# Softmax attention on TensorE: value products in groups of four slots instead of ones and twos

## The reference, cut to what matters

```python
q = (x @ Wq.T).reshape(B, S, H, hd).transpose(0, 2, 1, 3)     # k, v alike
att_rel_pos = jnp.einsum('bhsd,pd->bhsp', q, pos_emb_k)
att_idxs = jnp.clip(ar[None, :] - ar[:, None], -r, r - 1) % P  # r = 128, P = 256
att_pos = att_rel_pos[:, :, ar[:, None], att_idxs]
attn_val = jnp.einsum('bhqd,bhkd->bhqk', q, k)
att = jax.nn.softmax((attn_val + att_pos) * attn_scale, axis=-1)
y = jnp.einsum('bhqk,bhkd->bhqd', att, v)
```

## Time and profile before

| | us |
|---|---|
| median of three runs | 1145.63 |
| lowest and highest | 1142.08, 1151.29 |
| the profiled execution, its own time | 1143.02 |
| its span in the trace | 1141.1 |
| L1002, first to last start in the span | 439.5 to 898.0 |

### The profile page before, as it was taken

The page is one execution under the profiler, slowest core; times in us unless marked ns, Lnnn a source line. Parts: engine busy times, 40 slices in busy tenths (PEclk is TensorE's granted clock), DMA queues, the critical chain, the costliest instruction groups (busy, mean ns, idle before and its releaser), DMA issues. The chain is left out here.

```text
span 1141.1 us, 22305 instructions
## 1 busy us (share of the span) xinstructions
PE 1032.1 (90%) x7828; PEld 643.7 (56%) x7828; DVE 756.0 (66%) x1707; ACT 728.8 (64%) x1087; POOL 541.1 (47%) x707
## 2 busy tenths in 40 slices
PE   3699999999998758999999999999999889999997
PEld 2444444677785434555555555554444466878785
DVE  7135342478865566787788888877786257676766
ACT  1479988556555326777777777777775655545453
POOL 1257776575543231333355544444222277555564
PEclk9979999999999857999999999999999999999999
DMA  4621141544664497888888888887672576433333
GB/s 160 225 79 51 57 128 32 151 124 141 164 192 154 157 264 228 241 244 241 242 254 261 250 248 238 242 240 243 217 225 62 146 195 131 120 117 122 116 123 91
DMA packets 146430, 197.41 MB, mean 173 GB/s; under 512 B 33292, under 2 KB 113149, under 8 KB 146285
## 3 DMA queue, kind: packets, MB, share of 16 engines
q1 hardware_dynamic: 126254, 184.32, 52.7%
q0 software_dynamic: 20064, 11.66, 5.8%
HBM read 123.00 MB, written 72.74 MB: 172 GB/s over the span
## 5 line engine op out<-in xcount | busy, mean ns | idle before, releaser
L1089 DVE TENSOR_REDUCE a_part<-a_duo 128x2 f32<-128x1024 f32 (+3 forms) x256 | 215.3, 855 | 13.5 <-PE a_duo L962 11.9
L755 POOL DMA_DIRECT2D scr_y1c<-ys x240 | 118.9, 504 | 207.7 <-DVE ys L1070 204.8
L1082 DVE CUSTOM_DVE_ANT_0 a_band_sum<-a_duo,a_rel_raw 128x256 f32<-128x256 f32 (+2 forms) x320 | 131.4, 448 | 79.6 <-PE a_duo L962 59.2
L1526 POOL TENSOR_TENSOR f_hid_lo<-f_hid,att 128x512 fp32r<-128x512 f32 (+1 forms) x100 | 129.7, 1298 | 104.7 <-ACT att L1495 104.7
L706 ACT ACTIVATE a_probs<-a_duo 128x1024 f32<-128x1024 f32 x192 | 140.2, 828 | 25.5 <-PE a_duo L655 24.3
L975 PE MATMUL a_duo<-att 32*128 32x512 f32 (+3 forms) x672 | 138.1, 408 | 17.0 <-DVE a_part L1089 12.8
L962 PE MATMUL a_duo<-att 31*128 31x512 f32 (+3 forms) x672 | 144.8, 427 | 9.4 <-PEq L1131 4.3
L1042 ACT ACTIVATE a_rel<-a_rel_ps 128x384 f32<-128x384 f32 x240 | 117.5, 490 | 47.5 <-PE a_rel_ps L949 45.3
L1658 DVE TENSOR_TENSOR f_hid<-f_u,w_share 128x512 f32<-128x512 f32 (+1 forms) x168 | 116.3, 692 | 32.0 <-DMA w_share<-scr_cw 9.4
L644 POOL TENSOR_TENSOR a_probs<-a_probs,const 128x256 f32<-128x256 f32 x128 | 101.7, 811 | 60.9 <-ACT a_probs L706 60.8
L1526 POOL TENSOR_TENSOR f_hid_lo<-f_hid,f_hid_hi 128x512 fp32r<-128x512 f32 x68 | 87.9, 1292 | 79.7 <-ACT f_hid_hi L1495 79.6
(11 more groups left out here) (268 smaller groups left out, 2049.3 us busy)
## 6 DMA issues: line engine op xcount, KB each, us to landing
a_rel_raw<-scr_rel SPq DMA_DIRECT2D x128, 384.0 KB, 4.4
scr_rel<-a_rel SPq DMA_DIRECT2D x120, 384.0 KB, 3.6
w_share<-scr_cw SPq DMA_DIRECT2D x144, 128.0 KB, 3.1
w_share<-scr_cw SPq DMA_DIRECT2D x44, 256.0 KB, 3.2
scr_y1c<-ys POOLq DMA_DIRECT2D x240, 8.0 KB, 3.7
w_share<-scr_cw SPq DMA_DIRECT2D x20, 192.0 KB, 2.9
w_share<-scr_cw SPq DMA_DIRECT2D x16, 224.0 KB, 3.0
att<-scr_q SPq DMA_DIRECT2D x36, 96.0 KB
```

The costliest lines, as they stand in the source:

```text
L755: eng.dma_start(scr["y1c"][w, b, head, :, at:at + T // 4], sb["ys"][32 * (2 * hd + c) + HD * w:32 * (2 * hd + c) + HD * (w + 1), h % 2, :] ...
L1082: ins = dve.tensor_tensor_reduce(band_sum[:, m % 2, hd, 0:wide], both[:, hd, (a - 4 * x) * P:(b - 4 * x) * P], rel_raw[:, e % RING, hd, (a ...
L1089: ins = dve.tensor_reduce(part[:, h % 2, x, :, j % 4], both[:, :, lo * P:hi * P], AX.X, ALU.max, negate=True)
L1526: pool.tensor_tensor(hid_lo[0:m, n % 4, :], hid[0:m, n % 2, :], f32(hid_hi[0:m, n % 4, :]), ALU.subtract).then_inc(lo_ready, 1)
```

## The change

Values move between slots; no instruction is added or removed. Before, ten of the sixteen slots of a pair run one or two values, 2 in slots 0, 3, 5, 9, 12 and 14, and 1 in slots 1, 7, 8 and 10. Now four values run together at the end of each of the slots 2, 6, 10 and 14 (in slot 6 the values 0 to 3 of the pair, in slot 2 the last four of the pair before). VectorE's copy L1070 stands one slot later (slots 3 and 11 instead of 2 and 10).

```diff
-    VALUES = (2, 1, 0, 2, 0, 2, 0, 1, 1, 2, 1, 0, 2, 0, 2, 0)
+    VALUES = (0, 0, 4, 0) * 4
...
-                    while valued < min(n - 1 if n >= SLOTS else n // 16 * 16 + sum(VALUES[:n % 16 + 1]) - 3, SLOTS):
+                    while valued < min(n - 1 if n >= SLOTS else n // 16 * 16 + sum(VALUES[:n % 16 + 1]) - 4, SLOTS):
                         values(valued)
                         valued += 1
...
-                if (n - 3) % 8 == 7 and 0 <= n - 3 < SLOTS:
-                    h = (n - 3) // 8
+                if (n - 4) % 8 == 7 and 0 <= n - 4 < SLOTS:
+                    h = (n - 4) // 8
                     dve.wait_ge(pv_done, 8 * h + 8)
                     wait(dve, y_stored[h % 2], 128 * (h // 2))
                     dve.tensor_copy(ys[:, h % 2, :], acc[:, 0:QUARTER]).then_inc(y_saved, 1)
```

## The result

The changed kernel takes 1315.99 us (median of 4) against 1146.58 before: a ratio of 1.149, 95% interval 1.142 to 1.157. The direction was forecast, the size was not: +40 us forecast, +170 measured (1313.79 against 1143.02 in the profiled executions).

What follows compares the result with a forecast made beforehand. PE, DVE and ACT were taken as near each other, slots held by whoever is late. DVE, starved behind groups, adds 2.66 us a pair: 15.1 pairs give 40.2; 1143.0 + 40.2 - 0.5 = 1183 us, range 1160 to 1206.

Steps and rivals of the forecast that it cites:

- DVE is left without scores behind each group: Slots 2, 6, 10, 14: DVE idles a slot's length less 1.39 us; 5.45 us a pair after hiding two copies.
- The sum of a pair, 31.8 us: Stage, one pair: 22.99 DVE work + 5.45 + 1.96 + 1.4 = 31.8 us, against 29.14 before.
- The chain over L1107: Slots 3 and 11: next L949 waits for DVE's copy, DVE then for scores; 1.96 us a pair, stays.
- other idle time: DVE's remaining idle time in a pair: between 0 and about 3.2 us, taken as 1.4.
- The group cost of 0.13 us: PE's array-use change per value group; six fewer groups save 0.8 us a pair; rival that this decides: 1130.5 us, 5%.
- ACT's hold (the third rival): L1046 in slots 2, 6, 10 waits for a value's buffer; 0.5 us each, 23 more, 1206 us; 12%.
- so no clock is to be won: Stage: PE's granted clock is already 1.00, its upper level, so the change cannot raise it.
- L975's waits for L1089: Sign of being right: PE's L975 waits for DVE's maxima L1089 in most slots without values.
- The forecast of PE's busy time: Sign of being right: PE's busy time in a pair falls below 27 of 31.8 us.

## Why the prediction was right and where it failed

- **DVE is left without scores behind each group: right.** Its idle time there at full clock was 6.00 us a pair against 5.45.
- **The sum of a pair, 31.8 us: right for full clock.** 32.49 was measured, in a pair with 24.48 us of DVE work where the sum took 22.99 from a pair with less of the router's. The chain over L1107 left 0.82 and 0.60, 1.42 in all, of DVE idle time instead of 1.96; other idle time was 0.59 (32.49 - 24.48 - 6.00 - 1.42) instead of 1.4. That the total came so near is in part luck: two terms were 2.0 us too small together, two 1.4 too large. So 15.1 x (32.5 - 29.1) = 51 us are structure, where the forecast had 40. From copy to copy most pairs before take 29.3, by which it is 48. The run with 37 extra matmuls agrees: take off what its pairs are longer than 32.49, 0.86 x 15.1 = 13 us, and 1191 is left, against 1143 + 51 = 1194.
- **The group cost of 0.13 us: not decisive, as said.** By it groups of two would be 8 us slower than fours (four groups more a pair, 0.13 each, 16 pairs); they are 144 faster, and at full clock too a pair of theirs is shorter, 31.42 against 32.49.
- **ACT's hold (the third rival): refuted** by the two runs with seven buffers, above all the one at full clock. The prediction had the hold in three slots; by the code and the trace it is in four, slot 14 too. Hidden, it cost nothing.
- **The step that failed: "so no clock is to be won".** It asked only whether the clock could rise, and the sum then kept the prices of the earlier trace rows, all taken at 1.00, for a kernel that waits more. The clock fell to 0.73. Its own list had what was missing: L975's waits for L1089 in most slots without values. The other 170 - 51 = 119 us are this, some 8 us a pair: 41.1 against 32.5. The clock can account for it: at 0.73 it is at the lower level for 54% of the 540 us, 292 us, and half the clock can lose half of that at most, 146. The forecast of PE's busy time (below 27 us a pair) was the one that its profile refuted first: 36.02. No rival covered it, and the measured time lies 110 us above the range.

What stays open: which pattern of waits lowers the clock. Amount alone doesn't order the runs. The profile of before has three waits of 0.74 us of L949 for L1107 in the stage (at 779, 809 and 838 us), and its clock stays at 1.00; in the run with 15 extra matmuls the clock falls at 522.5 us, for one, behind rows that show no idle time. And all extra matmuls were whole-array ones in places where PE waits: whether they hold the clock by closing the waits or by the kind of work they are was not tried.

## What to carry to other kernels

When a change gives TensorE waits that it did not have, price it twice: at the clock of the profile, and with its matmuls at half of it, above all where a long run of matmuls follows the waits. Long groups on one engine starve the others by their length less what the buffers between them hold; groups of two instead of four cost 144 us less here, while spreading them further brought no gain that can be told. Useless matmuls in the waits are a quick test of whether lost time is clock.

## What the runs showed of the hardware

- The granted clock of the stage went from 1.00 to 0.73 by reordering the same instructions, and back to 1.00 by 37 extra matmuls a pair, 112 us faster. The extra 128x256 matmuls cost 0.11 us each (a group of three shows as 0.62 us, one of five as 0.84).
- With groups of two, PE's busy share of the stage was 89% at a clock of 1.00; with groups of four 88% at 0.73. The busy share of a profile does not tell the clock.
